# Graph network kernel: float32 gather tables and 64-node windows in two column halves, in place of three bfloat16 planes and 128-node tiles

## The chip, the cores and the metric

One core of one Trainium2 chip runs the whole program. The metric is the device time of one execution in microseconds (us), the median over several runs. The engines are PE (TensorE, matrix products; its weight loads stand apart as PEld), DVE (VectorE), ACT (ScalarE), POOL (GpSimd) and SP (SyncE, which here only issues DMAs).

## The reference, cut to what matters

N = 6250 nodes with 512 float32 features, E = 100000 edges, sorted by target node. Three layers each sum, for every node, the rows of the nodes that point to it:

```
dst = (6250 * uniform ** 2) as int, then sorted          # low nodes have many edges
x = layernorm(x + gcn(x) + time_embedding)               # layer 0
h = relu(mean_of_neighbours(x) @ Wl1.T + x @ Wr1.T + b1) # layer 1
y = mean_of_neighbours(h) @ Wl2.T + h @ Wr2.T + b2       # layer 2
out = layernorm(x + y)
```

The gcn layer scales rows by 1/sqrt(degree) on both sides and adds each node's own row. The sorted targets follow the square of a uniform number, so 391 * sqrt(t / 48.8) of the 391 groups lie in the first t tiles.

## The kernel before, in words

**Tiles and groups.** The nodes are cut into T = 49 tiles of 128. The sorted edges are cut into 391 groups of 256 (two halves of 128, CH = 2). For each layer L (0, 1, 2), POOL issues two indirect DMAs a group (L452), each of which fetches 128 rows of a table in memory by an index, into one of SLOTS = 10 buffers `raw`. That makes 2346 gathers in all. POOL waits for `slot_read[n]`, which PE raises when it has done with buffer n, so PE can be at most ten groups behind.

**Planes.** A row of a table is the float32 row split into three bfloat16 planes (high, middle, low) side by side, 3072 bytes. PE sums a group by six bfloat16 matmuls (`add_rows`, L1198): a 128x128 one-hot `oh` (which node of the tile does this edge go to) times 512 columns, for each of 2 halves and 3 planes. DVE makes the one-hots for five groups at a time (`half_block`, L763).

**End of a tile.** When the edges of a tile end within a group, PE's `tile_end` closes the sum, adds the group's edges again through `oh_next` into the other half of `sum_ps` (the sums lie in two PSUM banks in turn), weighs the sum of two tiles ago by W (`weigh`, L1206, eight float32 matmul instructions) and transposes the one before (`transpose_sum`, L1184). ACT copies the sum to `agg` with the scale (L920) and the transposed one to `aggT` (L902); DVE adds the product to X (`finish`, L673, L675) and normalizes (`norm`). With lags of up to six tiles, ACT and DVE then split the new rows into planes, and ACT stores the planes to the next layer's table, and the float32 rows beside them (L965, L974, L987). In layers 1 and 2 each node's own row is weighed too (`own_rows`: eight matmuls and four transposes, 50 rounds a layer, one for each five groups from the start of the layer).

**The order.** Each engine runs its own loop over the groups and jumps by counts of ended tiles (`ended`, `halves`). A new layer's gathers wait for the whole table of the layer before (`planes_stored`). In front of layer 0, after the degrees are counted, ACT and DVE make the planes of the first table in pairs of tiles (`stage`, L877, L634, L860, L626) and SP stores them (L361).

Of the kernel before, what the change touches and what calls it, by code (L numbers as in the profile page):

```python
# [5 lines left out]
def gnn_resnorm(nc, x, src, dst, t_emb, w0, b0, wt, bt, wl1t, wr1t, b1, wl2t, wr2t, b2, out):  # L6
    fp32, f32r, bf16 = mybir.dt.float32, mybir.dt.float32r, mybir.dt.bfloat16
# [5 lines left out]
    P = 128  # L13
# [5 lines left out]
    TILE_BITS = 63  # L19
    assert T + 1 <= TILE_BITS  # L20

# [9 lines left out]
    PLANES = 3  # L31
# [7 lines left out]
    FIN_LAG = 3  # L39
    DEV_LAG = FIN_LAG + 1  # L40
    NORM_LAG = DEV_LAG + 1
    STORE_LAG = NORM_LAG + 1
    ENDS = T - FIN_LAG - 1
    assert STORE_LAG == FIN_LAG + 3 and ENDS == T - 4
# [12 lines left out]
    with ctx:  # L57
# [20 lines left out]
        tile_base = sb("tile_base", [P, T + 1], fp32)  # L78
        ended = sb("ended", [1, 1 + NG], i32)
        halves = sb("halves", [1, 2 + NW], i32)  # L80
        end_at = sb("end_at", [1, T], i32)
# [8 lines left out]
        dinv2 = sb("dinv2", [P, T], fp32)  # L90
# [19 lines left out]
        next_hi_i = sb("next_hi_i", [P, EC], i32, early)  # L110
        next_hi = sb("next_hi", [P, EC], bf16, early)
# [9 lines left out]
        assert 4 * (NC + SB * P) <= 2 * SLOTS * CH * P + 2 * CH * P  # L121
        stage = sb("stage", [P, 2, BT, PLANES, D], bf16, mid)
        left_of = sb("left_of", [P, 2, 2, D], fp32, mid)
        cnt = sb("cnt", [P, T], fp32, mid)
        n_t = sb("n_t", [P, T], fp32, mid)
        end_t = sb("end_t", [P, T], fp32, mid)
        grp_f = sb("grp_f", [P, 2, T], fp32, mid)
        grp_i = sb("grp_i", [P, 2, T], i32, mid)
        grp_s = sb("grp_s", [P, 2, T], i32, mid)
        end_g = sb("end_g", [P, T], fp32, mid)  # L130
        iota_t = sb("iota_t", [P, T + 1], fp32, mid)
        iota_s = sb("iota_s", [P, SB], fp32, mid)
        pick = sb("pick", [P, SB + 1, T], fp32, mid)
        ended_s = sb("ended_s", [P, SB], fp32, mid)
        ended_w = sb("ended_w", [P, 1], fp32, mid)
        rooted_w = sb("rooted_w", [P, 2], fp32, mid)
        win_last = sb("win_last", [P, 1], fp32, mid)
# [7 lines left out]
        ended_h = sb("ended_h", [P, 1], fp32, mid)  # L145
# [3 lines left out]
        oh = sb("oh", [P, SLOTS, CH, P], bf16)  # L149
# [68 lines left out]
        def product(t1):  # L218

            return prod_ps[:, bass.ds((t1 % PR) * D, D)]  # L220

        def sums_of(L, t1, cols=D):

            return sum_ps[:, bass.ds(((t1 + T * L) % 2) * D, cols)]
# [1076 lines left out]
```

## Time and profile before

| | |
|---|---|
| median of 3 runs (lowest, highest) | 3285.66 us (3285.19, 3285.79) |
| span of the profiled execution | 3781.1 us |
| busy: PE, POOL, DVE, ACT | 81%, 59%, 30%, 13% of the span |
| mean granted TensorE clock | 0.905 of full |
| bytes moved by DMA | 1082.59 MB, 286 GB/s |

For the profiled execution only the span from its first to its last instruction is recorded, and no other time of its own; that span is 495 us longer than the median of the runs. So durations of single instructions are read from the profile, and sums are made against its 3781.1 us first and then carried to the median. A busy share does not tell what an engine waits for; the timeline and the waits do.

### The profile page before, as it was taken

How to read it: one execution, taken by the hardware profiler on the slowest of the kernel's cores; microseconds unless marked ns; L12 is line 12 of the kernel's file. 1: busy time of each engine (PE TensorE's matmuls, PEld its weight loads, DVE VectorE, ACT ScalarE, POOL GpSimd, SP SyncE). 2: the span in 40 equal slices, each digit the busy share in tenths (PEclk: the TensorE clock that was granted, in tenths of full speed). 3: DMA queues.
4: the chain of work that ended last, by engine and by line, in shares of the span. 5: the costliest groups of instructions: out<-in, count | busy, mean ns of one | idle time of the engine just before them, and what ended most of it. 6: DMA issues, size and time to landing. Idle time of an engine off the chain costs nothing.

```text
span 3781.1 us, 48502 instructions
## 1 busy us (share of the span) xinstructions
PE 3072.2 (81%) x12005; PEld 1387.0 (37%) x12006; DVE 1130.1 (30%) x1921; ACT 503.8 (13%) x1053; POOL 2244.1 (59%) x2367
## 2 busy tenths in 40 slices
PE   7266677788888877888999988897778889998888
PEld 7022223333333333334444433343334344443333
DVE  8701112333444431111222223332212222222223
ACT  0600000111112220000111111111000011111112
POOL 0166666666666636666666666655666666666663
PEclk9587778889899988899999998998889999999999
DMA  5787878888888868888889988988888888888885
GB/s 173 278 290 269 271 265 284 296 294 299 302 308 307 308 237 287 281 290 286 306 307 320 337 320 309 333 302 283 283 286 284 281 282 285 286 287 280 282 278 197
DMA packets 271564, 1082.59 MB, mean 286 GB/s; under 512 B 53146, under 2 KB 54716, under 8 KB 271506
## 3 DMA queue, kind: packets, MB, share of 16 engines
q0 software_dynamic: 187680, 922.63, 71.4%
q10 hardware_dynamic: 57294, 117.30, 8.5%
q1 hardware_dynamic: 26564, 42.34, 3.2%
q8 instruction: 13, 0.21, 0.0%
q14 instruction: 13, 0.11, 0.0%
HBM read 983.83 MB, written 99.06 MB: 286 GB/s over the span
## 4 chain that ended last, share of the span: by engine, by line
PE 63%; issue 16%; another core or an unknown queue 7%; POOL 5%; DVE 3%; ACTq 2%; DMA 1%; ACT 1%; DVEq 1%; POOLq 0%
PE sum_ps L1198 39%; PE prod_ps L1206 12%; PE root_ps L1206 9%; POOL raw L452 5%; PE aggT_ps L1184 2%; PE selfT_ps L1220 1%; PE root_ps L1115 1%; DMA raw<-table,idx_ring 1%; DVE left_of L634 1%; DVE stage L626 1%; DVE oh_hi L507 0%; ACT agg L920 0%; DVE oh L763 0%; ACTq L987 0%
## 5 line engine op out<-in xcount | busy, mean ns | idle before, releaser
L452 POOL DMA_INDIRECT raw<-table,idx_ring x2346 | 2234.7, 953 | 1412.5 <-issue 887.4
L1198 PE MATMUL sum_ps<-raw,oh 128*128 128x512 bf16 x7038 | 1756.2, 402 | 464.7 <-issue 370.5
L1198 PEld LDWEIGHTS sum_ps<-raw,oh 128*128 128x128 bf16 x7038 | 694.6, 102 | 1427.1 <-issue 772.4
L763 DVE TENSOR_TENSOR oh<-iota_ps,dst_rel 128x1280 bf16<-128x1280 f32 x237 | 352.8, 1489 | 1462.6 <-remote 1058.4
L1206 PE MATMUL prod_ps<-W,aggT 128*128 128x512 f32 x1152 | 552.8, 617 | 46.4 <-issue 45.7
L1206 PE MATMUL root_ps<-W,selfT 128*128 128x512 f32 x800 | 394.5, 637 | 64.2 <-issue 50.9
L1206 PEld LDWEIGHTS prod_ps<-W,aggT 128*128 128x128 f32 x1152 | 227.3, 198 | 297.9 <-issue 278.7
L902 ACT ACTIVATE aggT<-aggT_ps 128x512 f32<-128x512 f32 x144 | 86.0, 597 | 1568.9 <-remote 1035.4
L1198 PE MATMUL sum_ps<-raw,oh_next 128*128 128x512 bf16 x882 | 228.6, 393 | 31.8 <-issue 22.9
L1206 PEld LDWEIGHTS root_ps<-W,selfT 128*128 128x128 f32 x800 | 158.2, 203 | 257.4 <-issue 236.4
L942 ACT ACTIVATE selfT<-selfT_ps 128x512 f32<-128x512 f32 x100 | 59.7, 597 | 828.9 <-remote 526.7
L737 DVE CAST dst_end<-dst_tab 128x2 f32 x147 | 27.1, 185 | 444.3 <-remote 343.3
L1198 PEld LDWEIGHTS sum_ps<-raw,oh_next 128*128 128x128 bf16 x882 | 77.2, 99 | 132.1 <-issue 54.2
L1184 PE MATMUL aggT_ps<-ident,agg 128*128 128x128 f32 x588 | 95.6, 281 | 25.6 <-issue 20.7
L888 ACT ACTIVATE idx_ring<-idx_tab (+1 forms) x122 | 26.6, 219 | 669.8 <-remote 486.8
L1184 PEld LDWEIGHTS aggT_ps<-ident,agg 128*128 128x128 f32 x588 | 75.9, 145 | 106.7 <-issue 101.0
L675 DVE SCALAR_TENSOR_TENSOR X<-prod_ps,X (+1 forms) x98 | 67.3, 687 | 78.8 <-remote 52.3
L740 DVE TENSOR_SCALAR oh_next<-iota_row,tile_base,dst_end 128x128 bf16<-128x128 bf16 x294 | 80.8, 327 | 23.1 <-DVE dst_end L737 6.2
L655 DVE TENSOR_TENSOR X<-root_ps,b_all 128x512 f32 x49 | 33.8, 691 | 166.2 <-remote 106.9
L1115 PE MATMUL root_ps<-oh_hi,oh_lo 128*128 128x49 bf16 x782 | 75.0, 269 | 7.0 <-DVE oh_hi L507 6.6
L1115 PEld LDWEIGHTS root_ps<-oh_hi,oh_lo 128*128 128x128 bf16 x782 | 70.2, 142 | 11.7 <-DVE oh_hi L507 11.7
L1220 PEld LDWEIGHTS selfT_ps<-ident,selfbuf 128*128 128x128 f32 x404 | 51.3, 143 | 60.2 <-issue 58.6
(154 smaller groups left out, 1177.6 us busy)
## 6 DMA issues: line engine op xcount, KB each, us to landing
raw<-table,idx_ring POOLq DMA_INDIRECT x2346
table<-planes ACTq DMA_DIRECT2D x89, 384.0 KB
selfbuf<-rows ACTq DMA_DIRECT2D x103, 256.0 KB
table<-stage SPq DMA_DIRECT2D x21, 768.0 KB, 3.4
rows<-X ACTq DMA_DIRECT2D x49, 256.0 KB
X<-rows ACTq DMA_DIRECT2D x49, 256.0 KB
X<-in_x SPq DMA_DIRECT2D x6, 2048.0 KB
out<-X ACTq DMA_DIRECT2D x48, 256.0 KB
```

Source lines behind the costliest of these rows:

```text
L452: nc.gpsimd.indirect_dma_start(out=raw[:, n, j, :], out_offset=None, in_=tables[L][:, :], in_offset=bass.IndirectOffsetOnAxis(ap=idx_ring[ ...
L626: v.tensor_tensor(stage[:, b % 2, k:k + many, 2, :], left_of[:, n % 2, 0:many, :], stage[:, b % 2, k:k + many, 1, :], ALU.subtract).then_i ...
L675: v.scalar_tensor_tensor(tile_of_x(t1), product(t1), 1.0, tile_of_x(t1), ALU.mult, ALU.add, accum_out=column(sums, t1)).then_inc(S["prod_r ...
L740: made = v.tensor_scalar(oh_next[:, j, :], iota_row[:, :], tile_base[:, bass.ds(t1, 1)], dst_end[:, j:j + 1], ALU.add, ALU.is_equal)
L763: v.tensor_tensor(oh[:, which * HR:(which + 1) * HR, :, :].rearrange("p n j e -> p (n j) e"), iota_ps[:, 0:P].unsqueeze(1).to_broadcast([P ...
L902: a.activation(to[:, :], aggT_ps[:, :], ACT.Copy).then_inc(S["aggT_ready"], 1)
L942: a.activation(selfT[:, :], selfT_ps[:, :], ACT.Copy).then_inc(S["selfT_ready"], 1)
L1115: last = mm(hist_ps[:, 0:T], oh_lo[:, half, :, c], oh_hi[:, half, :, c], start=False, stop=False, skip_group_check=True)
L1184: last = nc.tensor.transpose(aggT_ps[:, k * P:(k + 1) * P], agg[:, k * P:(k + 1) * P], ident[:, :])
L1198: last = mm(bank, of[:, j, :], raw[:, n, j, p * D:(p + 1) * D], start=fresh, stop=False, skip_group_check=True)
L1206: last = mm(out_ps, xT[:, k * P:(k + 1) * P], W[:, n, k, :], start=(k == 0), stop=(k == KD - 1))
L1220: last = nc.tensor.transpose(selfT_ps[:, k * P:(k + 1) * P], rows[:, k * P:(k + 1) * P], ident[:, :])
```

## The change: what it does

**Tables.** All three tables hold float32 rows of 2048 bytes; the tables of layers 1 and 2 are the arrays `rows32` that were stored before as well. Nothing is split into planes. POOL still issues two gathers of 128 rows a group.

```diff
-        tables = [nc.dram_tensor(f"table{n}", [(T + (n == 0)) * P, PLANES * D], bf16, kind="Internal").ap() for n in range(NL)]
+        table0 = nc.dram_tensor("table0", [T * P, D], fp32, kind="Internal").ap()
         rows32 = [nc.dram_tensor(f"rows32_{n}", [(T + 3) * P, D], fp32, kind="Internal").ap() for n in range(1, NL)]
+        tables = [table0] + rows32
...
+                if many == 2:
+                    t = first + 1
+                    v.tensor_scalar(stage[:, b % 2, t % BT, :], X[:, t, :], dinv[:, t:t + 1], None,
+                                    ALU.mult).then_inc(S["staged_dve"], 1)
```

**Windows.** The nodes are cut into WT = 98 windows of 64. A one-hot has 64 columns and is float32. Edge half 0 of each group is summed in PSUM partitions 0 to 63 and half 1 in 64 to 127, both of the one bank `sum_ps`; at the end of a window ACT copies the upper half out and DVE adds the two into 64 rows of `agg`, without a scale (`finish` applies it). A tile ends with each second window: PE transposes then, and weighs the tile before in two parts, half at each window. `half_block` makes half as many columns.

```diff
+            def window_end(L, n, w1):
+
+                win = w1 + WT * L
+                mm(sum_ps[:, 0:1], zeros[:, :], zeros[:, 0:1], start=False, stop=True,
                    skip_group_check=True).then_inc(S["sum_ready"], 1)
-                pe.wait_ge(S["next_made"], tile)
-                pe.wait_ge(S["agg_ready"], tile)
-                add_rows(sums_of(L, t1 + 1), oh_next, n, True).then_inc(S["next_used"], 1)
-                with pe.If(t1 > 2):
-                    weigh(L, lagged(t1, 2))
+                with pe.If((w1 & 1) > 0):
+                    with pe.If(w1 > 2):
+                        weigh(L, tile_at(w1, 2), 0)
+                    pe.nop()
+                    add_next(n, win)
+                with pe.Else():
+                    with pe.If(w1 > 2):
+                        weigh(L, tile_at(w1, 2), 1)
+                    pe.nop()
+                    add_next(n, win)
+                    transpose_sum(L, tile_at(w1, 0))
                 pe.nop()
-                with pe.If(t1 > 1):
-                    if L == 0:
-                        pe.wait_ge(S["own_added"], lagged(t1, 1))
-                    transpose_sum()
-                pe.nop()
-
-            def transpose_sum():
-
+
+            def add_next(n, win):
+
+                pe.wait_ge(S["next_made"], win)
+                pe.wait_ge(S["agg_ready"], win)
+                add_rows(oh_next, n, True).then_inc(S["next_used"], 1)
+
+            def transpose_sum(L, t1):
...
+            def weigh(L, t1, half):
+
+                if half == 0:
+                    pe.wait_ge(S["wl_loaded"], 16 * (L + 1))
+                    pe.wait_ge(S["prod_read"], t1 + (T * L + LAG))
+                    pe.wait_ge(S["aggT_ready"], t1 + (T * L + LAG))
+                for k in range(half * KD // 2, (half + 1) * KD // 2):
+                    last = mm(product(L, t1), aggT[:, k * P:(k + 1) * P], W[:, 0, k, :], start=(k == 0),
+                              stop=(k == KD - 1))
+                if half == 1:
+                    last.then_inc(S["prod_ready"], 1)
+
+            def add_rows(of, n, fresh):
 
                 for j in range(CH):
-                    for p in range(PLANES):
-                        last = mm(bank, of[:, j, :], raw[:, n, j, p * D:(p + 1) * D], start=fresh, stop=False,
-                                  skip_group_check=True)
-                        fresh = False
+                    last = mm(sum_ps[j * H:(j + 1) * H, :], of[:, j, :], raw[:, n, j, :], start=fresh, stop=False,
+                              skip_group_check=True)
                 return last
...
+            def window_end(L, w1):
+
+                act.wait_ge(S["sum_ready"], w1 + WT * L)
+                a.activation(half_sum[:, :], sum_ps[H:P, :], ACT.Copy).then_inc(S["half_taken"], 1)
+                with act.If((w1 & 1) < 1):
+                    take_transposed(L, tile_at(w1, 0))
+                    with act.If(w1 > DEV_AT):
+                        (deviation, rectify, deviation)[L](L, tile_at(w1, DEV_AT))
                     act.nop()
-                with act.If(t1 > 1):
-                    take_transposed(L, lagged(t1, 1))
                 act.nop()
...
+            def add_halves(L, w1, h):
+
+                if h == 0:
+                    dve.wait_ge(S["aggT_done"], tile_at(w1, 0) + T * L)
+                dve.wait_ge(S["half_taken"], w1 + WT * L)
+                v.tensor_tensor(agg[h * H:(h + 1) * H, :], sum_ps[0:H, :], half_sum[:, :],
+                                ALU.add).then_inc(S["agg_ready"], 1)
```

**Stores.** SP, not ACT, issues the stores of the new rows, the reloads and the output, one by one in loops.

```diff
+            with sp.Fori(0, T) as t:
+                t1 = nc.s_assert_within(t + 1, 1, T, skip_runtime_bounds_check_because="a tile of the graph")
+                sp.wait_ge(S["norm_ready"], t1)
+                sp.dma_start(rows32[0][bass.ds(t1 * P - P, P), :], tile_of_x(t1)).then_inc(S["x_stored"], 16)
+            load_weights(0, wl1t, "wl_loaded")
```

The order of PE's instructions, in the part that runs when edges of a tile end within a group (each line a matmul, a wait or a register step; one float32 matmul of a line is two instructions on the engine). Before, a tile's end in layer 0:

```order
L1198 MATMUL sum_ps<-raw,oh 128x512 x6
L1255 REGISTER_ALU
L1255 UNCONDITIONAL_BRANCH
L1255 ISA
L1167 MATMUL sum_ps<-zeros 128x1
L1198 ISA
L1198 MATMUL sum_ps<-raw,oh_next 128x512 x6
L1172 COMPARE_AND_BRANCH
L1206 ISA
L1206 MATMUL prod_ps<-W,aggT 128x512 x4
L1172 UNCONDITIONAL_BRANCH
L1175 COMPARE_AND_BRANCH
L1184 MATMUL aggT_ps<-ident,agg 128x128 x4
```

Now a window's end, first the odd branch, then the even one and what follows:

```order
L1013 MATMUL sum_ps<-raw,oh 64x512 x2
L1069 REGISTER_ALU
L1069 UNCONDITIONAL_BRANCH
L969 MATMUL sum_ps<-zeros 128x1
L971 REGISTER_ALU x2
L971 COMPARE_AND_BRANCH
L972 COMPARE_AND_BRANCH
L1002 ISA
L1005 ISA
L1005 MATMUL prod_ps<-W,aggT 128x512 x2
L972 UNCONDITIONAL_BRANCH
L1013 MATMUL sum_ps<-raw,oh_next 64x512 x2
```

```order
L1005 ISA
L1005 REGISTER_ALU
L1005 MATMUL prod_ps<-W,aggT 128x512 x2
L977 UNCONDITIONAL_BRANCH
L1013 MATMUL sum_ps<-raw,oh_next 64x512 x2
L993 ISA
L995 MATMUL aggT_ps<-ident,agg 128x128 x4
L976 UNCONDITIONAL_BRANCH
L1069 REGISTER_ALU
L1069 COMPARE_AND_BRANCH
L1072 MATMUL sum_ps<-zeros 128x1
```

The six matmuls of a group have become two of 64 columns; the weighing of four lines has become two lines in each branch, ahead of the `oh_next` matmuls and no longer behind them; and the transposes stand in the even branch alone, directly behind `oh_next`.

ACT at the end of a tile before, in layer 0 (store of planes, transposed copy, scaled sum), and then now at a window's end:

```order
L987 DMA table<-planes 128x1536
L913 UNCONDITIONAL_BRANCH
L916 COMPARE_AND_BRANCH
L902 ACTIVATE aggT<-aggT_ps 128x512
L916 UNCONDITIONAL_BRANCH
L920 ISA
L920 ACTIVATE agg<-sum_ps,dinv 128x512
L927 COMPARE_AND_BRANCH
L949 ISA x2
L949 ACTIVATE selfT,sqsum<-X,sums 128x512
L952 REGISTER_ALU
L952 ACTIVATE root<-sqsum,eps 128x1
```

```order
L812 ACTIVATE half_sum<-sum_ps 64x512
L813 REGISTER_ALU
L813 COMPARE_AND_BRANCH
L801 ISA
L802 ACTIVATE aggT<-aggT_ps 128x512
L815 COMPARE_AND_BRANCH
L829 REGISTER_ALU
L830 ISA x2
L830 ACTIVATE junk,sqsum<-X,sums 128x512
L833 REGISTER_ALU
L833 ACTIVATE root<-sqsum,eps 128x1
```

The first thing that ACT does for a window is now the copy of the sum's upper half, and the issue of the store is gone from it.

SP's program behind the staging, which is new from its first loop on (the last rows are layer 1's store of the hidden rows and the reload of X):

```order
L344 UNCONDITIONAL_BRANCH
L344 ISA
L347 ISA x2
L347 DMA rows_1<-X 128x512
L344 REGISTER_ALU
L344 COMPARE_AND_BRANCH
L323 DMA W<-in_L_gnn_Wl 128x4x512
L350 UNCONDITIONAL_BRANCH
L350 ISA
L353 ISA
L354 ISA x2
L354 DMA rows_2<-hbuf 128x512
L355 ISA
L355 DMA X<-rows_1 128x512
L350 REGISTER_ALU
L350 COMPARE_AND_BRANCH
```

What ACT issued between its computations is now issued here, in the order of tiles.

## Rows read from the trace of the kernel before

**Rows 1.** the page's costliest groups: busy us, mean ns, idle before
```profile
L452 POOL DMA_INDIRECT raw<-table,idx_ring x2346 | 2234.7, 953 | 1412.5 <-issue 887.4
L1198 PE MATMUL sum_ps<-raw,oh 128*128 128x512 bf16 x7038 | 1756.2, 402 | 464.7 <-issue 370.5
```

**Rows 2.** timeline of POOL, 300 to 330 us: start, us, instruction, idle before it
```profile
300.01 0.95 POOL L452 DMA_INDIRECT raw<-table,idx_ring  x1 [0.30 <-issue]
301.26 0.94 POOL L452 DMA_INDIRECT raw<-table,idx_ring  x1 [0.30 <-issue]
...
328.51 0.94 POOL L452 DMA_INDIRECT raw<-table,idx_ring  x1 [3.43 <-remote]
```

**Rows 3.** timeline of POOL where each layer's gathers begin, and the last of all
```profile
174.22 1.10 POOL L452 DMA_INDIRECT raw<-table,idx_ring  x1 [78.24 <-issue]
...
1365.31 0.95 POOL L452 DMA_INDIRECT raw<-table,idx_ring  x1 [42.64 <-issue]
...
2574.20 0.94 POOL L452 DMA_INDIRECT raw<-table,idx_ring  x1 [41.31 <-DMA table<-raw]
...
3742.16 0.94 POOL L452 DMA_INDIRECT raw<-table,idx_ring  x1 [0.30 <-issue]
```

**Rows 4.** waits of POOL in the whole span: us, times, longest
```profile
POOL raw L452 <- remote: 467.2, 197, 5.3
```

**Rows 5.** the page's DMA queues: packets, MB, share of 16 engines
```profile
q0 software_dynamic: 187680, 922.63, 71.4%
```

**Rows 6.** windows of layer 0 early and layer 2 late: busy us, PEclk, DMA share, GB/s
```profile
300.00:400.00 100.00, 59.82 (x214) 20.87 (x215) 12.85 (x15) 1.34 (x4) 65.36 (x70) 0.80 0.80 271
3400.00:3700.00 300.00, 255.48 (x988) 113.04 (x985) 75.88 (x183) 47.73 (x115) 189.00 (x200) 0.93 0.82 279
```

**Rows 7.** timeline of PE, 344 to 361 us
```profile
356.73 0.59 PE L1198 MATMUL sum_ps<-raw,oh 128*128 128x512 bf16 x1 [2.21 <-issue]
358.13 0.61 PE L1198 MATMUL sum_ps<-raw,oh 128*128 128x512 bf16 x1 [0.81 <-issue]
```

**Rows 8.** timeline of layer 2's last tiles: PE alone
```profile
3742.74 5.34 PE L1198 MATMUL sum_ps<-raw,oh 128*128 128x512 bf16 x24
...
3747.95 1.46 PE L1198 MATMUL sum_ps<-raw,oh_next 128*128 128x512 bf16 x6
...
3749.24 3.60 PE L1206 MATMUL prod_ps<-W,aggT 128*128 128x512 f32 x8
...
3752.67 0.60 PE L1184 MATMUL aggT_ps<-ident,agg 128*128 128x128 f32 x4
...
3753.14 4.04 PE L1198 MATMUL sum_ps<-raw,oh 128*128 128x512 bf16 x18
```

**Rows 9.** timeline of the staging before the first gather
```profile
107.13 62.44 SPq L361 DMA_DIRECT2D table<-stage  x28
...
113.70 1.42 DVE L634 SCALAR_TENSOR_TENSOR left_of<-X,dinv,stage 128x512 f32<-128x512 f32 x2
...
115.03 1.22 DVE L626 TENSOR_TENSOR stage<-left_of,stage 128x1024 bf16<-128x1024 f32 x1
```

**Rows 10.** timeline of PE at the end of each layer
```profile
1337.80 1.46 PE L1198 MATMUL sum_ps<-raw,oh_next 128*128 128x512 bf16 x6
...
2548.87 1.45 PE L1198 MATMUL sum_ps<-raw,oh_next 128*128 128x512 bf16 x6
...
3757.05 1.46 PE L1198 MATMUL sum_ps<-raw,oh_next 128*128 128x512 bf16 x6
```

**Rows 11.** groups by shape, the operations of ACT and DVE that bear on a window
```profile
L902 ACT ACTIVATE aggT<-aggT_ps 128x512 f32<-128x512 f32 x144 | 86.0, 597 | 1568.9 <-remote 1035.4 <-PE aggT_ps L1184 314.1 <-issue 219.4
...
L655 DVE TENSOR_TENSOR X<-root_ps,b_all 128x512 f32 x49 | 33.8, 691 | 166.2 <-remote 106.9 <-issue 36.5 <-PE root_ps L1206 22.8
```

**Rows 12.** DMA issues of SP: KB each, median us to landing
```profile
rows<-zeros SPq DMA_DIRECT2D x6, 256.0 KB, 3.2
```

More of the change, by code:

```diff
@@ L38, in gnn_resnorm @@
     SORT_GAP = 6500
[L39 to L44, printed above, removed]
+    HID = 2
+    LAG = 3
+    FIN_AT, DEV_AT, NORM_AT = 3, 4, 6
     NL = 3
@@ L249, in ended_before @@
         def ended_before(which, g, groups):
             return nc.values_load_multi_w_load_instructions(
-                ended[0:1, bass.ds(g, groups + 1)], engines=[which], min_val=0, max_val=T,
-                skip_runtime_bounds_check_because="a count of the T tiles, made by a sum of T comparisons")[1]
+                ended[0:1, bass.ds(g, groups + 1)], engines=[which], min_val=0, max_val=WT,
+                skip_runtime_bounds_check_because="a count of the windows, made by a sum of as many comparisons")[1]
@@ L261, in last_half @@
         def last_half(which):
             return nc.values_load_multi_w_load_instructions(
-                halves[0:1, NW:NW + 2], engines=[which], min_val=0, max_val=T,
-                skip_runtime_bounds_check_because="a count of the T tiles, made by a sum of T comparisons")[1]
+                halves[0:1, NW:NW + 2], engines=[which], min_val=0, max_val=WT,
+                skip_runtime_bounds_check_because="a count of the windows, made by a sum of as many comparisons")[1]
         def rooted_before(which, b):
@@ L271, in rooted_before, with tile_at, each @@
                 skip_runtime_bounds_check_because="held between 0 and T + 1 when it is made")[1]
-        def lagged(t1, lag):
-            return nc.s_assert_within(t1 - lag, 1, T, skip_runtime_bounds_check_because="the first tiles are left out")
-        def each(eng, first, end, part, most=T):
+        def tile_at(w1, lag):
+            return nc.s_assert_within(((w1 + 1) >> 1) - (lag + 1) // 2, 1, T, skip_runtime_bounds_check_because="the first windows are left out")
+        def each(eng, first, end, part, most=WT):
             with eng.If(end > first):
-                with eng.Fori(first & TILE_BITS, end) as t:
-                    part(nc.s_assert_within(t + 1, 1, most, skip_runtime_bounds_check_because="a tile of the graph"))
+                with eng.Fori(first & WIN_BITS, end) as w:
+                    part(nc.s_assert_within(w + 1, 1, most, skip_runtime_bounds_check_because="a window or tile of the graph"))
                 eng.nop()
@@ new lines, in _ @@
+            load_weights(0, wl2t, "wl_loaded")
+            with sp.Fori(0, T - 1) as t:
+                t1 = nc.s_assert_within(t + 1, 1, T - 1, skip_runtime_bounds_check_because="not the last tile")
+                sp.wait_ge(S["norm_ready"], t1 + T)
+                sp.dma_start(out[bass.ds(t1 * P - P, P), :], tile_of_x(t1)).then_inc(S["out_stored"], 16)
+            sp.wait_ge(S["norm_ready"], 2 * T)
+            sp.dma_start(out[(T - 1) * P:N, :], X[0:TAIL, T - 1, :]).then_inc(S["out_stored"], 16)
```

593 lines of the change are left out of this document (194 added, 399 removed).

## The prediction

> **What bounds the kernel now.** I read the costliest groups first. PE has the largest busy share, but the longest group of all is POOL's gathers: 2346 of them at 953 ns [rows 1]. So I turned to POOL's timeline. Where nothing holds it, it begins a gather every 1.25 us, 0.95 busy and 0.30 between, and never sooner, though buffers are free; from time to time it stands still for some us, for something outside itself [rows 2]. The waits give 467 us of such standing in 197 pieces [rows 4]. The only semaphore there is `slot_read`, so POOL waits for PE to free a buffer.
>
> The account of the profiled span follows. The first gather begins at 174.2; the idle times ahead of layers 1 and 2 are 42.6 and 41.3; the last gather ends at 3743.1, 38.0 before the end [rows 3]. 2346 gathers at 1.25 are 2932 (less 0.3 for each layer's last gap). Together that is 3227.7, and the 553 that are left are POOL's stalls.
>
> Is the transfer the bound? The gather queue takes 71.4% of 16 engines [rows 5], 0.714 * 3781 / 2346 = 1.15 us a gather, near POOL's 1.25 but under it, and with all queues the engines are 80 to 82% busy early and late alike [rows 6]. Fewer bytes alone then give little.
>
> Is PE the bound? A float32 matmul instruction begins every 3.43 / 8 = 0.43 us and a bfloat16 one every 0.216. A tile's end late in layer 2: 24 matmuls (four groups) and everything to the next group take 10.40, of which the groups 5.21 (1.30 each) and the end 5.19: `oh_next` 1.29, weighing 3.43, transposes 0.47 [rows 8]. POOL needs 10.0 for four groups. So PE is the slower one only where tiles are short. Tile t has about 28 / sqrt(t) groups (56 in front, 4 at the end).
>
> But the profile also has stretches like [rows 7]: matmul records 1.4 us apart in place of 0.22, some of them missing, in a part with a mean granted clock of 0.80 of 2.4 GHz [rows 6]. They empty into POOL's stalls. The median of the runs is 3285.7, 495 below the span. 3227.7 plus 58 gives it. I conclude that POOL's 1.25 holds without the profiler too, and that most of the stalls don't: unprofiled, the kernel is 98% POOL's pace, beginning and ends. I make the sum on the span's own parts, and carry to the median with 58 us of stalls in place of 553.
>
> **The change, part by part.**
>
> *Gathers.* Count and rows a gather are the same, the bytes fall from 3072 to 2048 a row. POOL's part is writing one request a row; I take 1.25 unchanged (lower bound: the 0.95 falls with the bytes to 0.63, 0.93 in all; a rival below). 2932 stay.
>
> *Staging.* Stores run from 107.1 to the first gather at 174.2, at DVE's pace: 1.42 + 1.22 a pair, about 1.3 a tile for 49 tiles [rows 3, 9]. Now ACT takes 28 tiles and DVE 21 with one operation each, under 20 us; then the stores bind. 19.3 MB in 67 us was 288 GB/s, so 12.8 MB take at most 45 us and at least the 20 of the computing. I take 37: **-30** (-22 to -47).
>
> *Ends of layers.* From the last `oh_next` to the next layer's first gather, or to the end: 27.5, 25.3, 24.1 [rows 3, 10]. Now: half a weighing 1.7, `oh_next` 1, transposes 0.5, copy 0.6, weighing 3.4, DVE 0.7, four short steps 2, the last store 3.2 [rows 8, 11, 12], and some ten handovers of 0.15: 14.5. No three tiles of planes follow. **-13, -13, -10** (half or double that as bounds). ACT's stores move to SP, whose queue has only them; they were hidden, and are.
>
> *Groups on PE.* Two float32 matmuls are four instructions, 1.72 us, if they run one after the other. The trace has no matmul into half the columns beside another, so the bounds are 1.72 and, if the two halves overlap, 0.86 (the second instruction of half 0 beside the first of half 1, and the second of half 1 beside the next group's first). Before: 1.30. Both end below POOL's 2.5, so in long tiles it costs nothing; the cover is the 2.5, and it is gone in short tiles. I take 0.86: different columns, different PSUM partitions, different inputs. In the Trainium skill, TensorEngine Tiling, Key Properties says that tiles operate independently and run matmuls in parallel, which no row here shows; its other point, that a change of tiling mode drains the engine, speaks against this change, since each window changes mode four times. By the first alone a group would be 0.86; the second would add to the window, which is bounded next.
>
> *Windows.* 98 ends instead of 49. Each costs half a weighing 1.72, `oh_next` 0.86, and x. In x are: twice 0.43 for an instruction of half 1 that has nothing beside it, at the end of the groups and of `oh_next`; the drains when PE changes between 64 and 128 columns, each between nothing and the 0.402 - 0.216 = 0.19 by which a matmul's duration exceeds its pitch [rows 1, 8]; and what the round trip PE, ACT, DVE, PE outlasts the half weighing. The trip is 0.60 + 0.69 [rows 11] plus three handovers, 1.75 against 1.72, so hidden if ACT and DVE are free. x is 0.5 to 1.9; I take 0.86 + 0.1 + three times 0.08 = 1.2. A tile: 2 * (1.72 + 0.86 + 1.2) + 0.47 = 8.03, before 5.19.
>
> PE is late from the tile where its time exceeds POOL's. Layer 0: 0.86G + 8.03 = 2.5G at G = 4.9, tile 33, group 320. From there 71 * 0.86 + 16.3 * 8.03 = 192 against 178: +14. Layers 1 and 2 also weigh own rows, 3.43 + 0.47 for each five groups up to group 250, 0.78 a group: G = 9.3, tile 9, group 169; 222 * 0.86 + 81 * 0.78 + 39.9 * 8.03 = 574 against 555: +19 each. The same reckoning for before (1.30G + 5.19) gives +3, +6.5, +6.5. Difference **+36**.
>
> *Stalls left.* Of the 58, part is PE with its clock down: a group then takes twice 1.30, over 2.5. Twice 0.86 is under. I take half away: **-28** (0 to -58).
>
> *The rest:* one-hots half as wide (1489 ns a block before) and no planes free ACT and DVE, which wait most of the time; nothing.
>
> **Sum:** 3285.7 - 30 - 36 + 36 - 28 = 3228; I say **3225**. On the profiled span the same terms hold, and its stalls may fall by more, since PE has a third fewer instructions in a group.
>
> **The rivals.**
>
> A, the forecast: halves overlap, round trip hidden. 3120 to 3300. Chance 0.52.
>
> B, halves overlap, but the round trip isn't hidden: one PSUM bank, so PE can't begin the next window's sum before ACT and DVE have taken this one, and ACT may be inside a square or a copy (0.6 to 0.7) when the sum closes. For it: before, two banks took turns; against it: the weighing now stands in front of the wait. With x = 1.9 a tile is 9.43, and the layers lose 44, 77, 77: 3285.7 - 66 + 198 - 16 - 28 = 3374, slower. It decides from x = 1.55 up. Chance 0.16.
>
> C, halves run one after the other: 1.72 a group, x = 0.4, a tile 8.15. Layer 0 is PE's from tile 7, +153; layers 1 and 2 wholly, 391 * 1.72 + 195 + 399 = 1267 against 978, +289 each: 3285.7 - 66 + 731 - 16 - 28 = 3907, slower. For it: the trace shows PE's instructions strictly in a row, and float32 takes two a matmul. Chance 0.19.
>
> D, partial overlap, some 1.2 a group (weight loads in the way): +66, +112, +112, about 3480; 3400 to 3640. Chance 0.06.
>
> E, POOL's price falls with the bytes to 0.93: PE then bounds, layers 827, 924, 924, with 144 in front, 86 behind and some stalls: about 2935, up to 3100. Against it: the 0.95 is the same where the engines are busy and where they aren't. Chance 0.07.
>
> **How the numbers follow.** Within 0.2% is 3279 to 3292, about what a measurement of this kernel can tell from no change. A reaches it with 0.05 of its 0.52 and passes it with 0.02. Faster: 0.45 of A and all of E, 0.52; same 0.05; slower B, C, D and A's rest, 0.43. A's own range is 3120 to 3300. The range for 8 in 10 takes A, B, D and half of E: 3060 to 3640; C is left out.
>
> **What would show it.** POOL's gathers still 1.25 apart, 0.95 each (else E). First gather near 144. In a backlog, groups of four float32 instructions 0.86 apart, starts of two of them nearly together (1.72: C). From a window's closing matmul to `oh_next` no more than 1.9 us, ended by no wait (else B). Idle ahead of layers 1 and 2 near 30. The forecast is wrong above all if the first sight of PE's pairs is one behind the other.

## The result and the profile after

The changed kernel takes **3338 us** (median of 4 runs, 3335.6 to 3342.1), the kernel before 3285.7 in the same comparison: ratio 1.016, 95% interval 1.0145 to 1.0173. It is slower by 52 us; the forecast was 3225, faster. In two later comparisons the ratio was 1.0159 (1.0142 to 1.0176) and 1.0146 (1.0128 to 1.0164).

In some sessions every kernel takes 16 to 24% longer (the same chip ran the kernel before in 3818 us once and in 3285 once), and as the profile behind [rows 1 to 12], with its span of 3781 us, looks like one of these, the ledger below is drawn from a second profile of the unchanged kernel before, of 3284 us (run f0).

The page of the kernel after: the lines for the gathers of layers 1 and 2 and for PE's sums of whole groups (columns as in [rows 1]):

```profile
L433 POOL DMA_INDIRECT raw<-rows,idx_ring x1564 | 1486.9, 951 | 676.7 <-issue 561.3
L1013 PE MATMUL sum_ps<-raw,oh 128*64 128x512 f32 x4692 | 1243.1, 652 | 347.2 <-DMA raw<-table,idx_ring 154.5
```

A gather still takes POOL 951 ns (953 before) with a third fewer bytes. POOL's timeline of the kernel after at the layer edges (to be read beside [rows 3]):

```profile
140.07 1.10 POOL L433 DMA_INDIRECT raw<-table,idx_ring  x1 [43.18 <-issue]
...
1125.45 0.94 POOL L433 DMA_INDIRECT raw<-table,idx_ring  x1 [0.30 <-issue]
...
1164.56 0.94 POOL L433 DMA_INDIRECT raw<-rows,idx_ring  x1 [38.17 <-issue]
...
2233.32 0.94 POOL L433 DMA_INDIRECT raw<-rows,idx_ring  x1 [41.93 <-DMA rows<-hbuf]
...
3288.99 0.94 POOL L433 DMA_INDIRECT raw<-rows,idx_ring  x1 [0.30 <-issue]
```

The same view of the kernel before in its second profile:

```profile
174.33 1.10 POOL L452 DMA_INDIRECT raw<-table,idx_ring  x1 [78.25 <-issue]
...
1164.12 0.95 POOL L452 DMA_INDIRECT raw<-table,idx_ring  x1 [0.30 <-issue]
1201.93 0.94 POOL L452 DMA_INDIRECT raw<-table,idx_ring  x1 [36.85 <-issue]
...
2244.52 0.94 POOL L452 DMA_INDIRECT raw<-table,idx_ring  x1 [39.83 <-DMA table<-raw]
...
3243.89 0.95 POOL L452 DMA_INDIRECT raw<-table,idx_ring  x1 [0.30 <-issue]
```

From such rows comes the ledger, in us. A layer's phase runs from the start of its first gather to the end of its last; 782 gathers at 1.25, less the last gap, would be 977.2.

| | until first gather | layer 0 | idle | layer 1 | idle | layer 2 | tail | span |
|---|---|---|---|---|---|---|---|---|
| before (f0) | 174.3 | 990.7 | 36.9 | 1002.8 | 39.8 | 1000.3 | 37.6 | 3282.4 |
| after | 140.1 | 986.3 | 38.2 | 1026.8 | 41.9 | 1056.6 | 43.9 | 3333.9 |
| i1, additions early | 140.2 | 987.4 | 38.1 | 1026.9 | 42.0 | 1042.4 | 42.3 | 3319.2 |
| h2, all three | 140.1 | 987.2 | 40.7 | 1011.1 | 43.5 | 1017.5 | 45.0 | 3285.1 |
| i3, with one read | 140.1 | 981.6 | 33.5 | 988.6 | 42.5 | 992.5 | 43.6 | 3222.3 |
| i2, one own product | 140.0 | 986.5 | 38.1 | 991.5 | 40.3 | 1010.9 | 42.3 | 3249.7 |
| i4, before, edited | 174.2 | 988.2 | 38.3 | 996.7 | 40.5 | 999.0 | 38.4 | 3275.3 |

The first gather is 34 us earlier and layer 0 costs 3 less with the idle time behind it. **Layer 1 costs 24 more, layer 2 56 more**, and the idle times behind them 2 and 6.

Where in the layers? Four stretches of the kernel after: POOL's groups 179 to 269 of layer 1 and of layer 2 (the first two lines), then the last 88 groups of layer 1 and the last 74 of layer 2. The columns are those of [rows 6]: start and end, length, busy time of PE, PEld, DVE, ACT and POOL, granted clock, DMA share, GB/s.

```profile
1612.00:1865.00 253.00, 233.15 (x844) 83.21 (x846) 68.43 (x146) 39.78 (x74) 169.95 (x180) 0.98 0.74 228
2683.00:2955.00 272.00, 240.35 (x849) 86.14 (x847) 89.14 (x208) 45.44 (x98) 172.83 (x180) 0.96 0.67 200
1950.00:2190.00 240.00, 214.07 (x789) 67.16 (x788) 78.37 (x183) 44.40 (x83) 165.64 (x176) 0.95 0.75 232
3080.00:3315.00 235.00, 208.32 (x757) 65.23 (x757) 93.90 (x252) 51.95 (x117) 139.09 (x148) 0.93 0.63 186
```

180 gathers at 1.25 are 225 us; they took 253 and 272. PE is busy 233 and 240 of that, so it is the late one, and it still idles 20 and 32 us (26 and 27 in the lower two rows). PE's idle time in all, by what ended it, kernel after (total, times, longest):

```profile
PE sum_ps L1013 <- issue: 122.1, 52, 4.3
PE root_ps L1020 <- issue: 74.3, 32, 4.0
PE root_ps L1020 <- DVE X L631: 48.5, 23, 4.2
...
PE sum_ps L1013 <- DVE oh L707: 32.2, 29, 2.4
PE sum_ps L1013 <- DVE agg L658: 10.4, 7, 1.7
```

And one such place in layer 2, PE's timeline:

```profile
2794.57 1.08 PE L1013 MATMUL sum_ps<-raw,oh_next 128*64 128x512 f32 x4
2795.58 0.66 PE L995 MATMUL aggT_ps<-ident,agg 128*128 128x128 f32 x4
2796.07 0.17 PE L1072 MATMUL sum_ps<-zeros 128*128 128x1 bf16 x1
2800.32 2.07 PE L1020 MATMUL root_ps<-W,selfT 128*128 128x512 f32 x2 [4.08 <-DVE X L631]
```

beside DVE's:

```profile
2793.48 0.68 DVE L658 TENSOR_TENSOR agg<-sum_ps,half_sum 64x512 f32<-64x512 f32 x1 [1.73 <-ACT half_sum L812]
...
2795.02 0.82 DVE L707 TENSOR_TENSOR oh<-iota_ps,dst_rel 128x640 f32<-128x640 f32 x1
2798.50 0.69 DVE L628 TENSOR_TENSOR X<-b_all,X 128x512 f32 x1 [2.66 <-issue]
2799.23 0.69 DVE L631 TENSOR_TENSOR X<-root_ps,X 128x512 f32 x1
```

PE has the next own-row round ready, but `root_ps` still holds the round before. DVE adds that only behind the last window's end, the one-hots and 2.66 us in which it waits for nothing shown; by the program it reads its counts of ended windows there. Elsewhere PE itself stands 1.8 to 4.3 us at a block start with "issue" as the reason. In layer 1 and in the last groups of layer 2 such pieces come about every 27 us, once per block of ten groups; in layer 2's groups 179 to 269, where DVE's late addition ends most of them, about every 16, once per half block.

### The profile page after: what moved, and what is told of

It is laid out like the page before. It is cut to its first block, busy times and chain, and to the rows that moved or that the text cites. A ratio compares the mean times of both kernels' runs of the same rounds, so it can differ in the third digit from the quotient of the medians.

```text
span 3333.9 us, 49595 instructions
## 1 busy us (share of the span) xinstructions
PE 2787.5 (84%) x10248; PEld 953.9 (29%) x10250; DVE 1071.1 (32%) x2318; ACT 493.6 (15%) x1044; POOL 2245.6 (67%) x2367
## 4 chain that ended last, share of the span: by engine, by line
PE 58%; issue 14%; POOL 12%; DMA 6%; DVE 4%; DVEq 3%; ACT 2%; POOLq 0%; ACTq 0%; SPq 0%
PE sum_ps L1013 30%; POOL raw L433 12%; PE prod_ps L1005 12%; PE root_ps L1020 11%; DMA raw<-table,idx_ring 3%; PE aggT_ps L995 2%; DMA raw<-rows,idx_ring 2%; ACT half_sum L812 1%; PE root_ps L915 1%; PE selfT_ps L1034 1%; PE sum_ps L969 1%; DVEq L246 1%; DVE oh L707 1%; DVEq L234 1%; DVE X L631 1%
## 5 line engine op out<-in xcount | busy, mean ns | idle before, releaser
L433 POOL DMA_INDIRECT raw<-rows,idx_ring x1564 | 1486.9, 951 | 676.7 <-issue 561.3
L1013 PE MATMUL sum_ps<-raw,oh 128*64 128x512 f32 x4692 | 1243.1, 652 | 347.2 <-DMA raw<-table,idx_ring 154.5
L433 POOL DMA_INDIRECT raw<-table,idx_ring x782 | 748.4, 957 | 281.1 <-issue 264.0
L658 DVE TENSOR_TENSOR agg<-sum_ps,half_sum 64x512 f32<-64x512 f32 x294 | 200.9, 683 | 1291.8 <-ACT half_sum L812 1291.6
L1013 PEld LDWEIGHTS sum_ps<-raw,oh 128*64 128x64 f32 x4692 | 295.7, 143 | 966.0 <-issue 950.9
L812 ACT ACTIVATE half_sum<-sum_ps 64x512 f32<-64x512 f32 x294 | 174.4, 593 | 1083.8 <-PE sum_ps L969 1080.8
L1013 PE MATMUL sum_ps<-raw,oh_next 128*64 128x512 f32 x1176 | 318.7, 620 | 10.4 <-DVE agg L658 10.4
L707 DVE TENSOR_TENSOR oh<-iota_ps,dst_rel 128x640 f32<-128x640 f32 x237 | 194.5, 821 | 275.3 <-PE sum_ps L1013 220.4
L686 DVE TENSOR_SCALAR oh_next<-iota_row,win_base,dst_end 128x64 f32<-128x64 bf16 x588 | 162.8, 331 | 44.3 <-DVE dst_end L683 19.1
L1013 PEld LDWEIGHTS sum_ps<-raw,oh_next 128*64 128x64 f32 x1176 | 58.6, 135 | 234.3 <-issue 234.3
```

The costliest lines, as they stand in the source:

```text
L433: nc.gpsimd.indirect_dma_start(out=raw[:, n, j, :], out_offset=None, in_=tables[L][:, :], in_offset=bass.IndirectOffsetOnAxis(ap=idx_ring[ ...
L658: v.tensor_tensor(agg[h * H:(h + 1) * H, :], sum_ps[0:H, :], half_sum[:, :], ALU.add).then_inc(S["agg_ready"], 1)
L686: made = v.tensor_scalar(oh_next[:, j, :], iota_row[:, 0:H], win_base[:, bass.ds(w1, 1)], dst_end[:, j:j + 1], ALU.add, ALU.is_equal)
L707: v.tensor_tensor(oh[:, which * HR:(which + 1) * HR, :, :].rearrange("p n j e -> p (n j) e"), iota_ps[:, 0:H].unsqueeze(1).to_broadcast([P ...
L812: a.activation(half_sum[:, :], sum_ps[H:P, :], ACT.Copy).then_inc(S["half_taken"], 1)
L1013: last = mm(sum_ps[j * H:(j + 1) * H, :], of[:, j, :], raw[:, n, j, :], start=fresh, stop=False, skip_group_check=True)
```

## The experiments

Runs e1 to e4 stood beside a kernel before of 3825 us and g1 to g4 beside one of 3818. The changed kernel itself was not measured there, so they rank among themselves only. The others stood beside a kernel before of 3285 to 3288.

### f0 and f1: both kernels again, unchanged

> The kernel before, unchanged, for a profile on the same chip as the others of this call: the page of it that I read had a span 495 us over the median of its runs, and its stalls came with pieces of idle time that no event explains; the four kernels of the first call, on another chip, showed the same (stalls of 250 to 320 us a layer, POOL waiting for a remote event) and the kernel before took 3825 us there. Theory 1: the inflation belongs to the chip and not to the kernel. Where the kernel before takes near 3286 us, its profile has POOL stalls of 20 to 70 us in all, and phases of 980 to 1010 us a layer. Rival: recording the profile inflates this kernel, and the span is again near 3780 beside a median near 3286.

> The changed kernel, unchanged, as the base of this call. Where the kernel before takes near 3286 us: 3338, ratio 1.016. On a chip where it takes near 3825 us: if that chip slows PE's part by a fixed share, 3850 to 3900, ratio 1.01 to 1.02; if it slows each handover between engines, the changed kernel with twice as many window ends loses more, 4000 to 4100, ratio 1.05 to 1.07.

Measured: before 3284.2 (span 3282.4), after 3339.7, ratio 1.0159. Theory 1 of f0 holds in the main: the inflation was not the kernel's own. It was not the chip's either, since one chip gave both times. Its phases are 1003 and 1000 us in layers 1 and 2; the 58 us of stalls that I had carried to the median are 62 here (990.7 + 1002.8 + 1000.3 less 3 * 977.2).

### e1 and f2: PE reads its counts group by group

```diff
-                    ends = ended_before(mybir.EngineType.PE, b * SLOTS, SLOTS)
-                    if L > 0:
-                        rounds = rooted_before(mybir.EngineType.PE, b)
                     for n in range(SLOTS):
...
-                        group(b, n, ends[n], ends[n + 1])
+                        ends = ended_before(mybir.EngineType.PE, b * SLOTS + n, 1)
+                        group(b, n, ends[0], ends[1])
```

> The changed kernel, but PE reads its counts of ended windows group by group (two numbers ahead of each group, two more ahead of each half block's own rows) in place of eleven and three numbers at the start of each block of ten groups. Theory 1 (block starts): in the stretches in which POOL stalls, PE idles 1.8 to 4.3 us once in about 27 us, where a block starts, with no releaser, because its sequencer reads 14 numbers there with nothing queued behind it on the array; spread out they lie under the matmuls. Then 2 to 3 us for each of some 45 blocks in which PE is the late one come back: 3338 becomes 3220 to 3260. Theory 2 (the windows' own work, and the round trip PE, ACT, DVE, PE): the idle time at the blocks is slack that is given back anyway: 3325 to 3345. Theory 3 (DVE's root additions and one-hots hold PE at those places, not PE's own reads): no change, 3330 to 3345.

> The changed kernel, PE reading its counts group by group in place of fourteen at the start of each block of ten groups (the first run of it was on a chip where the base was not measured). Theory 1 (block starts, PE idle 1.8 to 4.3 us every 27 us in the stall zones): 80 to 120 us under the base of this call. Theory 2 (the windows' own work and the round trip): within 10 us of the base. Against both: if a read in the middle of a block holds PE's sequencer longer than the 0.86 us of a group, the reads are paid twice over, 20 to 100 us above the base.

Measured: e1 4086; f2 3325.7, 14 under f1 (1.0112 against 1.0159), not 80 to 120. (Its profile is of the longest of its four runs, 3333.8.) PE's idle pieces ahead of `root_ps` with "issue" fell from 74 to 15 us, but DVE's part stayed (43 and 11), and ahead of `sum_ps` 234 short pieces of 127 us together stood in place of 54 of 122. Spreading alone moved the waiting. Theory 1 in this form was wrong; theory 2's "within 10" nearly right.

### e2: the counts read twice

```diff
+                    ended_before(mybir.EngineType.PE, b * SLOTS, SLOTS)
                     ends = ended_before(mybir.EngineType.PE, b * SLOTS, SLOTS)
```

> The changed kernel with PE's eleven counts of a block read twice at each block's start, the first reading not used. Theory 1 (block starts): each block in which PE is late costs 2 us more, some 45 to 60 of the 120 blocks: 3400 to 3460. Theories 2 and 3 (windows' work, or DVE): the reads lie beside other waits, 3335 to 3350.

Measured 4101, 15 above e1 with its spread reads, both beside 3825. Without a time of the changed kernel beside it, it decides nothing.

### e3 and f3: two PSUM banks for the sums

```diff
-        sum_ps = pb("sum_ps", [P, D], fp32)
+        sum_ps = pb("sum_ps", [P, 2 * D], fp32)
...
+                with pe.If((first & 1) > 0):
+                    part(1)
+                with pe.Else():
+                    part(0)
```

> The changed kernel with two PSUM banks for the sums, in turn by window: oh_next of a window no longer waits until ACT and DVE have taken the sum that it ends; the transposes at a tile's end do. PE has one branch more for each group. Theory 1 (block starts): PE's waits for DVE's agg are 10.4 us in all, so -10 to +15, 3328 to 3353. Theory 2 (the round trip is what is lost, 196 windows of layers 1 and 2 and the tail of layer 0, some 0.3 to 0.6 each): -50 to -90, 3250 to 3290.

> The changed kernel with two PSUM banks for the sums in turn by window, and one branch more for each group on PE. Theory 1: the round trip is nearly hidden (PE waits 10 us in all for it), so -10 to +15 against the base of this call. Theory 2 (round trip): -50 to -90. If what a slower chip adds is paid at each handover between PE, ACT and DVE, the gain is larger there than on the faster chip.

Measured: e3 4009, the lowest of the e and g runs; f3 3353.3 (1.0194), 14 above f1: the branch a group costs more than the second bank gives. Since a source of waits can look worthless while others stand behind it (below), f3 alone does not refute rival B. PE's list does: it waits for DVE's `agg`, the end of the round trip, 10.4 us in all in the kernel after, and still only 18.0 in i3, where most of the other waits are gone.

### g4: both halves in the same 64 partitions

```diff
-                    last = mm(sum_ps[j * H:(j + 1) * H, :], of[:, j, :], raw[:, n, j, :], start=fresh, stop=False,
+                    last = mm(sum_ps[0:H, :], of[:, j, :], raw[:, n, j, :], start=fresh and j == 0, stop=False,
```

> The changed kernel with both edge halves summed in the same 64 PSUM partitions (the upper 64 stay zero). If the trace's pairs of matmuls that start together are what makes a group 0.86 us, a group now takes 1.72, and PE bounds all layers: 3850 to 3950. If the pairs are an artefact of the records, nothing changes: 3338.

Measured 4251 (one run, beside 3818), so its time says little. Its PE timeline settles the question. From the first of 24 instructions (six groups) to the closing are 10.44, 1.74 a group. The kernel after runs the instructions in pairs: two groups take 1.87 and three 2.73 (from 2789.91 to 2792.64), so 0.86 a group:

```profile
525.24 10.51 PE L1013 MATMUL sum_ps<-raw,oh 128*64 128x512 f32 x24
535.68 0.18 PE L969 MATMUL sum_ps<-zeros 128*128 128x1 bf16 x1
```

### g1 and i1: DVE adds the own row's product one half block earlier

```diff
-                with dve.If(r > 1):
-                    prev = nc.s_assert_within(r - 1, 1, T, ...)
-                    dve.wait_ge(S["root_ready"], r + (T + 1) * (L - 1))
+                with dve.If(r < T + 1):
+                    prev = nc.s_assert_within(r + 0, 1, T, ...)
+                    dve.wait_ge(S["root_ready"], r + ((T + 1) * (L - 1) + 1))
```

> The changed kernel, but DVE adds the own row's product of round r in the half block in which PE makes it, ahead of that half block's window ends, in place of one half block later. Theory 1a (what the block starts showed is mostly PE waiting for DVE's late additions and one-hots, which come behind the last window end of the half block before; in layer 2 two additions stand there): 25 to 45 us under the changed kernel, so 3295 to 3315 where the kernel before takes 3288, and most of it in layer 2. Theory 1b (PE's own reads of its counts): under 8 us. Theory 2 (PE's work at the windows is the whole loss, the waits are slack): under 8 us.

> The changed kernel with DVE's additions of the own rows' product ahead of the window ends, nothing else. They are 56 us of PE's waits in the trace. Theory 1 with DVE as the main source: 20 to 35 us under the changed kernel (ratio to the kernel before 1.005 to 1.010), most of it in layer 2. If the sources lie behind one another, each worth little alone: 5 to 15 us.

Measured: g1 4112 (4099 without one run of 6435); i1 3319.2, ratio 1.0094, 17 to 21 under the changed kernel. PE's waits for DVE's X are gone from its list (55 us), but those with "issue" ahead of `root_ps` grew from 74 to 109: behind DVE stood PE's own reads. Between the two expectations.

### g2: the next half block's one-hots ahead of the window ends

```diff
                     for half in range(2):
+                        half_block(1 - half, ...)
                         if L > 0:
                             each(dve, rounds[half], rounds[half + 1], lambda r: own_rows(L, r), T + 1)
                         each(dve, ends[half], ends[half + 1], window_end)
-                        half_block(1 - half, ...)
```

> The changed kernel, but DVE makes the next half block's one-hots ahead of this half block's window ends in place of behind them. PE waits 32 us in all for one-hots, half of it where it is late anyway. Theory 1a: 10 to 20 us under the changed kernel, at the ends of the layers above all. Theory 2: none. Against both: oh_next of the first window comes 0.8 us later, and costs up to 0.3 us at some 60 windows, +0 to +15.

Measured 4179, 67 to 80 above g1. What it does alone where the kernel before takes 3286 was not measured.

### g3 and h2: all three edits, and h1, their base

> The changed kernel with the early additions, the early one-hots, and PE's reads group by group. Theory 1 (PE idles some 100 us in the stretches in which POOL stalls, and all three causes lie behind one another, so that taking one away alone uncovers the next): 60 to 95 us under the changed kernel, 3245 to 3280 where the kernel before takes 3288, layer phases of 990 to 1015 us. Theory 2: 3325 to 3345.

> The changed kernel, unchanged, as the base. Where the kernel before takes near 3286: ratio 1.014 to 1.018. Where it takes near 3820, the variants of it so far stood at ratios of 1.047 to 1.093 to the kernel before, so 1.06 to 1.09.

> The changed kernel with DVE's additions of the own rows' product and its one-hots ahead of the window ends, and PE's reads group by group. Theory 1 (idle pieces of PE at block starts, one behind the other): 60 to 95 us under the base of this call, ratio to the kernel before 0.99 to 1.00 where that takes near 3286. Theory 2 (PE's work at the windows): within 15 us of the base.

Measured: g3 4068; h1 3336.5; h2 **3286.3**, 50 under h1 and the same as the kernel before (1.000, 0.999 to 1.001). Less than the 60 to 95 of theory 1, far outside theory 2's 15. The phases of layers 1 and 2 fell by 21 and 42 from h1's 1032 and 1060. PE's timeline of h2 at the end of layer 0 shows what is left, a gap behind each window in which PE reads two counts for the next group:

```profile
1109.87 0.17 PE L1077 MATMUL sum_ps<-zeros 128*128 128x1 bf16 x1
1110.84 1.94 PE L1019 MATMUL sum_ps<-raw,oh 128*64 128x512 f32 x8 [0.80 <-issue]
...
1121.60 0.17 PE L1077 MATMUL sum_ps<-zeros 128*128 128x1 bf16 x1
1122.70 1.97 PE L1019 MATMUL sum_ps<-raw,oh 128*64 128x512 f32 x8 [0.93 <-issue]
```

### i3: one read a group in place of two

```diff
-                        ends = ended_before(mybir.EngineType.PE, b * SLOTS + n, 1)
-                        group(b, n, ends[0], ends[1])
+                        if n == 0:
+                            first, end = ended_before(mybir.EngineType.PE, b * SLOTS, 1)
+                        else:
+                            first, end = end, ended_by(mybir.EngineType.PE, b * SLOTS + n)
+                        group(b, n, first, end)
```

> The changed kernel with the early additions and one-hots, and PE reading one number a group in place of two (the end of one group is the start of the next). The gaps of 0.2 to 0.9 us behind each window, 1.1 us a tile in the tail, shrink by the 0.3 that a read costs: 15 to 30 us under the version with two reads, 3255 to 3270, ratio 0.991 to 0.996. Rival: PE's matmuls are the bound there and the gaps are branches, not reads: within 5 us of it, ratio 0.998 to 1.001.

Measured **3226.9** (3224.1 to 3231.2), ratio 0.9827 (0.9811 to 0.9843): the fastest of all, 111 under the changed kernel and 58 under the kernel before. Against h2 the one read was worth 59, twice the most that I expected. PE's waits in h2, then in i3:

```profile
PE sum_ps L1019 <- issue: 91.0, 205, 1.9
PE sum_ps L1019 <- DVE oh L713: 47.8, 36, 1.5
PE root_ps L1026 <- issue: 30.3, 70, 0.9
```

```profile
PE sum_ps L1025 <- issue: 50.5, 88, 1.9
PE sum_ps L1025 <- DVE oh L719: 43.0, 36, 1.5
PE root_ps L1032 <- issue: 22.5, 54, 0.8
```

48 us of idle pieces are gone, and the ledger has the gain where PE was late: 22 and 25 in layers 1 and 2, 13 around layer 0's end. That is more than the 48; PE's busy time is 44 less as well (2795.1 to 2751.3), for the same matmuls.

### i2 (and e4): less work in the own rows, waits as they are

```diff
-                by_weights(root_ps[:, :], selfT, 1, S["root_ready"])
+                mm(root_ps[:, :], selfT[:, 0:P], W[:, 1, 0, :], start=True, stop=True).then_inc(S["root_ready"], 1)
```

This kernel leaves out three of the four products of each node's own row.

> The changed kernel with one of the four products of each node's own row (two of eight matmul instructions); so layers 1 and 2 lack three quarters of the own-row product. It takes 2.8 us from each of 100 rounds of PE, 0.55 us a group up to group 250, and leaves the waits and block starts. Theory 1: the first stall zones of layers 1 and 2 (POOL's gathers 358 to 538 of each layer, some 24 and 45 us) go, the second ones (328 groups on) stay: -60 to -80, 3260 to 3280. A theory by which POOL's stalls come from elsewhere than PE's lateness (a transfer that lands late, ACT's index copies): under 10 us.

> The changed kernel with one of four products of each node's own row, so layers 1 and 2 lack three quarters of it; PE's waits and reads stay. It takes 2.8 us of PE's work from each of 50 rounds a layer, some 45 us from the stretch in which PE is the later one (groups 169 to 250). Theory 1 and 2 alike: the stalls of groups 180 to 270 go, 30 to 35 us in layer 1 and 45 to 50 in layer 2; the tail's 20 a layer stay. Ratio 0.990 to 0.996. If more than the tail's is left, the waits do not hang on PE's load.

Measured: e4 4029; i2 3254.8, 0.9914 (0.9897 to 0.993), as expected: layer 1's phase 35 shorter, layer 2's 46, though the mean granted clock is lower (0.90 against 0.92). So the waits are no law of their own. PE's work and its idle pieces add up, and what exceeds POOL's pace becomes a stall, whichever of the two is cut.

### i4: the kernel before with the same edits

> The kernel before with the same three edits: additions and one-hots ahead of the tile ends, one read a group. On the faster chip its POOL stalls 19 and 16 us in layers 1 and 2 and PE is 10 us late at the ends. If PE's waits are its stalls too: 15 to 35 us less, ratio 0.990 to 0.995, and the two designs differ by the 34 us of the first table less the ends. If its stalls come from elsewhere: 0.998 to 1.002.

Measured 3282.6, 0.9991 (0.9981 to 1.0): 2 us. Where the kernel before is late, in groups 179 to 269, it is late by its work: PE is busy 240 of 243 us there (the line of f0 below), so the edits find next to no idle time to take. In the whole run they do not come for free either: i4 has 48 us in which PE waits for DVE's `oh_next`, which stands nowhere in f0's waits.

## Why the prediction was wrong

**The bound** was read rightly: POOL's 1.25 a gather did not move with the bytes, so rival E fell.

**Staging:** forecast -30, first gather near 144; measured -34, 140.1.

**Ends of layers:** the chain was right. From the last `oh_next` to the next layer's first gather I had 14.5; the rows give 1151.22 to 1164.56, 13.3, against 27.2 before (1174.73 to 1201.93). But the idle time ahead of layer 1 is 38, not near 30, since PE begins that `oh_next` 25 us behind the last gather (9.7 before). The sum counted this lateness as a term of its own, and for layer 0 it held: -2 forecast, -3 measured.

```profile
1149.33 1.96 PE L1005 MATMUL prod_ps<-W,aggT 128*128 128x512 f32 x4
1151.22 1.08 PE L1013 MATMUL sum_ps<-raw,oh_next 128*64 128x512 f32 x4
```

**Groups:** forecast 0.86, and rival C (1.72) fell. A tile of four groups late in layer 1, PE's timeline of the kernel after (to be read beside [rows 8]):

```profile
2131.72 1.94 PE L1013 MATMUL sum_ps<-raw,oh 128*64 128x512 f32 x8
2133.59 0.18 PE L969 MATMUL sum_ps<-zeros 128*128 128x1 bf16 x1
2133.63 1.96 PE L1005 MATMUL prod_ps<-W,aggT 128*128 128x512 f32 x4
2135.53 1.08 PE L1013 MATMUL sum_ps<-raw,oh_next 128*64 128x512 f32 x4
2136.53 0.66 PE L995 MATMUL aggT_ps<-ident,agg 128*128 128x128 f32 x4
2137.03 0.17 PE L1072 MATMUL sum_ps<-zeros 128*128 128x1 bf16 x1
...
2142.38 1.94 PE L1013 MATMUL sum_ps<-raw,oh 128*64 128x512 f32 x8 [0.27 <-DVE oh L707]
```

Without the last 0.27 the tile is 10.39, and less 4 * 0.86 it is 6.95, where I had 8.03: **the window's x was 0.66, not 1.2**. The rows say where it lies: two groups take 1.87 instead of 1.72, half a weighing 1.90 instead of 1.72, `oh_next` 1.00 instead of 0.86, the closing and the last small matmul 0.13 to 0.21 together. An instruction with nothing beside it costs 0.15 more, not 0.43.

The Trainium skill, TensorEngine Tiling (Array Packing), Key Properties, says that tiles run in parallel and that a change of mode drains the engine. By the first the trace agrees: 0.86 a group, against 1.74 in g4. Of the second no row here gives a price; all four changes of a window lie within its 0.66.

**The step that failed** is "PE late": I took PE's time as the sum of its matmuls and round trips, and left out that PE stands still at block and half-block starts. Here are the same groups, 179 to 269, cut by PE's own matmuls: layers 1 and 2 of the kernel after, then of i3, then layer 1 of the kernel before (f0), with the columns as above:

```profile
1630.77:1882.94 252.17, 232.32 (x842) 82.44 (x838) 68.97 (x149) 39.50 (x74) 169.17 (x179) 0.97 0.74 228
2706.95:2975.47 268.52, 236.81 (x842) 84.00 (x839) 90.74 (x215) 45.63 (x100) 171.85 (x179) 0.96 0.68 201
1609.95:1846.42 236.47, 227.31 (x842) 81.19 (x838) 70.86 (x148) 39.52 (x74) 178.31 (x190) 1.00 0.82 254
2644.46:2882.88 238.42, 227.79 (x842) 81.76 (x839) 91.46 (x213) 45.64 (x100) 177.54 (x188) 1.00 0.79 235
1669.21:1911.95 242.74, 239.82 (x969) 114.27 (x968) 77.55 (x125) 38.20 (x74) 169.74 (x178) 1.00 0.98 358
```

POOL needs 225 for them. The matmuls of the kernel after are 227 when little else is in the way (i3), near the 222 that my formula gives with x = 0.66 (236 with 1.2). In the kernel after they took 252 and 269: 20 and 32 us of idle time, and 5 and 9 us more busy time for the same instructions. The latter goes with the clock. In the stretches in which POOL stalls the granted clock falls to 1.2 GHz 19 times, and each time during an idle piece of PE of 2.0 us or more, or right behind it. One of them, the 2.01 us ahead of 1658.4 and what follows:

```profile
1655.50:1658.40 2.90, 0.93 (x6) 0.05 (x2) 0.59 (x3) 0.22 (x1) 2.28 (x3) 1.00 0.86 231
1658.40:1662.50 4.10, 4.06 (x6) 1.75 (x7) 0.00 (x0) 0.00 (x0) 2.89 (x4) 0.58 0.90 305
```

With the waits taken away (i3) the clock of these groups is 1.00. So a wait is paid for twice, by itself and by the slower matmuls behind it.

With all this, layers 1 and 2 with the idle time behind them cost 26 and 63 more than before where I had about 0 and 2.5. These 26 and 60, the 28 below, less 5 for staging and layer 0, are 109 of the 113 between forecast and result; the rest lies in rounding and between the profiles and the medians.

**Stalls left:** I took away half of 58 (-28) since a PE with its clock down would keep POOL's pace. Nothing came: the phases hold 9, 50 and 79 us over 977 now. The 58 were not that. Of the 26 and 23 us over 977 that the kernel before has in layers 1 and 2, 21 and 17 lie in groups 179 to 269, where its clock is 1.00 and PE is busy for all but 2 to 3 us. They are its own work, for which my sum had +6.5 a layer. That sum was wrong: it added up all groups from PE's first lateness on as one, and let PE's faster end pay back what POOL had lost before, though POOL cannot catch up. The kernel before has a mean granted clock of 0.98, the kernel after 0.92.

What the runs put in place of the step: PE's idle pieces have three sources (DVE's late addition to `root_ps`, DVE's one-hots, PE's reads), and each stands behind another. Alone, spread reads gave 14 and early additions 17 to 21; together with the one-hots 50, and with half the reads 111. With most of them away the change comes out at 3227, beside the forecast of 3225. That nearness is luck: i3 is another kernel than the one forecast, x was forecast too high, and the stalls that I took away were of another kind.

## What to carry to other kernels

A design that cuts an engine's work into twice as many steps must be costed with the time in which that engine does no work at each step: register reads, branches, and the wait for the partner that comes behind its own such steps. Look for idle pieces at a fixed distance (here 27 us, one block) in the stretch in which the producer stalls; if several sources stand there, take them away together, or each will look worthless. Look at the granted clock right behind such pieces: here the matmuls paid for them a second time. Ask also whether the profile comes from the same condition as the time that you explain.

## What the runs showed of the hardware that was not expected

Where the kernel before takes 3820, PE's records and what follows from them part. In g4, PE's closing matmul of a window, and ACT's copy of that sum, 8.8 us behind it, though ACT had been idle for 15:

```profile
569.33 0.18 PE L969 MATMUL sum_ps<-zeros 128*128 128x1 bf16 x1
```

```profile
578.26 0.59 ACT L812 ACTIVATE half_sum<-sum_ps 64x512 f32<-64x512 f32 x1 [15.21 <-remote]
```

Over the 294 windows of the kernel after this distance is 0.04 us at the median and 1.6 at most; in e1 a quarter of them lie over 3.9, the longest at 19.9, 706 us in all (13 in the kernel after). In g4, with its halves one behind the other, it is 129 us in all. POOL's gathers keep their 1.25 between its stalls. Why PE's completions come late there is open; that a kernel with twice as many closings suffers more from it (ratios of 1.05 to 1.09 where the kernel before takes 3820) fits, but was not tried with the changed kernel itself.

The weight of a register read surprised me too. With one read a group instead of two, PE's list has 133 idle pieces and 48 us less, and the whole kernel gained 59, as POOL waits for PE there. What one read costs by itself was not measured.
